# A time-mix and expert-mix block on one core: weights split in place, a new load order ahead of the routed experts, and a combination cut in two

## What is computed

```
mod = (silu(c) @ wmod).reshape(4, 6, 1, -1); sa, ca, ga, sb, cb, gb = six parts   # ga, gb kept away from 0
h  = layernorm(x) * (1 + ca) + sa
x  = x + ga * attn(h)
h  = layernorm(x) * (1 + cb) + sb
x  = x + gb * ffn(h)

attn: time mix    xr, xk, xv = mixes of LN(h) and LN(h) one row earlier
                  r = sigmoid(xr @ Wr); k = xk @ Wk; v = xv @ Wv;  h += (r * exp(u+k)*v / (exp(u+k)+1e-8)) @ Wout
      channel mix h += sigmoid(x2r @ Wr2) * (relu(x2k @ Wk2)**2 @ Wv2)
ffn:  shared expert  (silu(x Wsg) * (x Wsu)) @ Wsd, hidden width 704
      routed experts 8 of width 352, softmax router, each row goes to its best 2, weighted sum
```

## Time and profile before

| | before |
|---|---|
| median of 3 runs | 1906.12 us (1905.55 to 1906.73) |
| profiled execution, its own time | 1902.73 us |
| its span, first to last instruction | 1901.0 us |
| mean granted TensorE clock in it | 0.956 |
| PE busy / DVE busy / ACT busy / POOL busy | 1726.2 / 1347.9 / 767.5 / 548.4 us |

### The profile page before, as it was taken

One profiled execution on the slowest core, in us unless ns is written; L12 is line 12 of the kernel. 1 busy time (PEld: TensorE's weight loads), 2 busy tenths in 40 slices (PEclk: granted clock), 3 DMA queues, 4 the chain that ended last, 5 costly groups with the idle time before them and its releaser, 6 DMA issues.

```text
span 1901.0 us, 28565 instructions
## 1 busy us (share of the span) xinstructions
PE 1726.2 (91%) x9093; PEld 1494.5 (79%) x9093; DVE 1347.9 (71%) x2468; ACT 767.5 (40%) x1147; POOL 548.4 (29%) x631
## 2 busy tenths in 40 slices
PE   4599999997678999999999884999999999997898
PEld 0488888885567878878878784999999999986888
DVE  4899999984587788777776533667666666756752
ACT  2333333341334545545454212455554545432221
POOL 0344444441354434545545420000000000006620
PEclk8699999999789999999999996999999999999999
DMA  9422222211533434545545786766667676677731
GB/s 333 144 91 88 88 88 88 88 66 67 180 111 124 143 139 150 200 151 192 206 147 183 272 287 187 251 237 242 240 233 251 230 255 230 247 243 246 244 118 45
DMA packets 141362, 338.74 MB, mean 178 GB/s; under 512 B 20649, under 2 KB 20649, under 8 KB 135777
## 3 DMA queue, kind: packets, MB, share of 16 engines
q1 hardware_dynamic: 110592, 250.15, 38.4%
q10 hardware_dynamic: 20448, 54.01, 7.7%
q0 software_dynamic: 10240, 33.56, 5.1%
HBM read 230.14 MB, written 107.53 MB: 178 GB/s over the span
## 4 chain that ended last, share of the span: by engine, by line
PE 65%; DVE 19%; DMA 5%; issue 4%; POOL 3%; ACT 2%; SPq 1%; another core or an unknown queue 0%; DVEq 0%; ACTq 0%; POOLq 0%
PE bank L566 16%; PE bank L567 15%; PE bank L568 15%; DVE mix L1544 6%; PE bank L577 4%; PE bank L2032 4%; PE bank L2034 4%; PE bank L2033 4%; PE bank L2027 2%; DVE xm_lo L1550 1%; DMA base<-xres_rows 1%; ACT xm_hi L1147 1%; POOL diff L1000 1%; DMA stage<-in_w_k 1%; DVE k_lo L1557 1%
## 5 line engine op out<-in xcount | busy, mean ns | idle before, releaser
L566 PE MATMUL bank<-gu_hi,ex_x_hl 128*128 128x352 f32 x1136 | 380.3, 335 | 2.7 <-DVE gu_lo L1810 1.9
L568 PE MATMUL bank<-gu_hi,ex_x_hl 128*128 128x352 f32 x1136 | 368.0, 324 | 0.0
L567 PE MATMUL bank<-gu_lo,ex_x_hl 128*128 128x352 f32 x1136 | 367.9, 324 | 0.0
L1081 POOL DMA_INDIRECT raw<-expert_out_rows,out_slots x64 | 74.2, 1159 | 624.7 <-DMA expert_out_rows<-y_rows 588.4
L1628 DVE TENSOR_TENSOR hid<-bank,sg_t 128x352 f32<-128x352 f32 x142 | 74.0, 521 | 231.6 <-ACT sg_t L1205 225.3
L566 PEld LDWEIGHTS bank<-gu_hi,ex_x_hl 128*128 128x128 f32 x1136 | 215.7, 190 | 3.4 <-DVE gu_lo L1810 2.1
L1544 DVE SCALAR_TENSOR_TENSOR mix<-diff,vecs,h2T 128x128 f32<-128x128 f32 x256 | 160.7, 696 | 80.0 <-POOL diff L1000 80.0
L567 PEld LDWEIGHTS bank<-gu_lo,ex_x_hl 128*128 128x128 f32 x1136 | 215.8, 190 | 0.0
L568 PEld LDWEIGHTS bank<-gu_hi,ex_x_hl 128*128 128x128 f32 x1136 | 215.1, 189 | 0.0
L2032 PE MATMUL bank<-dn_hi,hid_hi 128*128 128x512 f32 x426 | 172.7, 405 | 23.5 <-DVE hid_lo L1632 17.2
L1205 ACT ACTIVATE sg_t<-bank 128x352 f32<-128x352 f32 x142 | 66.1, 465 | 306.8 <-PE bank L568 290.7
(11 more groups left out here) (229 smaller groups left out, 3942.0 us busy)
## 6 DMA issues: line engine op xcount, KB each, us to landing
raw<-in_ex_gu SPq DMA_DIRECT2D x39, 1408.0 KB, 6.6
raw<-in_ex_dn SPq DMA_DIRECT2D x39, 512.0 KB, 7.4
ex_x<-expert_in_rows SPq DMA_DIRECT2D x78, 256.0 KB, 2.7
expert_out_rows<-y_rows ACTq DMA_DIRECT2D x78, 256.0 KB, 5.4
h_rows<-h_t SPq DMA_DIRECT2D x64, 256.0 KB, 2.4
h_turned<-h_hl ACTq DMA_DIRECT2D x32, 512.0 KB
ex_x_hl<-h_turned ACTq DMA_DIRECT2D x32, 512.0 KB
x_t<-in_x SPq DMA_DIRECT2D x32, 256.0 KB, 2.6
```

Source lines behind the costliest of these rows:

```text
L566: pe.matmul(acc, act_hi[i], w_hi[i], start=(i == 0), stop=False)
L567: pe.matmul(acc, act_hi[i], w_lo[i], start=False, stop=False)
L568: last = pe.matmul(acc, act_lo[i], w_hi[i], start=False, stop=(i == chunks - 1))
L1081: pool.indirect_dma_start(rows[:, pair % 2, a, :], None, ys_d, bass.IndirectOffsetOnAxis(ap=out_slots[:, k, n:n + 1], axis=0)).then_inc(ar ...
```

## The change

Four things change.

**The opening.** Weights are no longer staged: each is loaded to the place of its own low part (`plain[w]` lies where `w_*_lo` lies), ACT writes the high part, and DVE subtracts in place. So no weight waits for a buffer, and the splits are spread: DVE splits r and k in step -2 of the time mix, v in step -1, o in step 0, and the three channel weights and the router's in steps 3 to 5. The modulation rows are spread too: GA and SB in step -4, CB in step 0, GB in step 1. PE's r no longer waits for all splits. SP's order of loads is new.

**Ahead of the routed stage** SP issues the first expert before the pads, and the first rows right behind the pads; the second expert and the 14 base loads follow.

**In the routed stage** SP's steps are written out instead of looped, and the base and residual loads (28 of 256 KB) go one into each step.

**The combination** is cut in two: `weighted` (both, gated) stands ahead of DVE's `hid` of the half, `combined` (the residual) stays behind it; everything is one tile later. ACT's order is the same.

```diff
 def combined_at(q):
-    return SPLIT + 1 + q // 2, q % 2
+    return SPLIT + 2 + q // 2, q % 2
...
             for i in range(2, len(W1)):
-                load_weight(i)
-            sp.wait_ge(mod_out, 32)
-            for b in range(B):
-                sp.dma_start(flat(mod1[:, b]), mod_d[b, 0:2 * D].partition_broadcast(P)).then_inc(mod1_in, 16)
...
+            sp.wait_ge(mod_out[0], 32)
+            load_mod1(0)
+            load_weight(2)
+            load_weight(3)
+            for b in range(1, B):
+                load_mod1(b)
+            sp.wait_ge(*lnh_vec.done(0, "scaled"))
+            sp.dma_start(x_t[:, 0, :], x_d[2 * P:3 * P, :]).then_inc(x_in[0], 16)
...
             def scaled(t):

                 batch = t.n // TPB
+                if t.pair is None and t.n < 2:
+                    dve.wait_ge(*((mod1_in, 16) if t.n == 0 else (mod1_later, 16 * (B - 1))))
...
             sp.wait_ge(route_done, 1)
+            load_expert(FIRST)
             sp.wait_ge(pads_zero, 1)
             for e in range(E):
                 pad_rows(e)
-            for first in range(2):
-                load_expert(ROUTED.tile(first))
-            sp.wait_ge(rs_out, 16 * FU)
-            for n in range(FU):
-                if n >= 2:
-                    sp.wait_ge(fb_in[n % 2], 16 * (n // 2))
-                sp.dma_start(base[:, n, :], xres_d[n * P:(n + 1) * P, :]).then_inc(fb_in[n % 2], 16)
...
+            load_rows(FIRST)
+            load_expert(ROUTED.tile(1))
+            sp.wait_ge(rs_out, 16 * FU)
...
+            def time_step_and_weights(t):
+                time_step(t)
+                if t.only(-4):
+                    mod_row(GA)
+                    mod_row(SB)
+                if t.only(-2):
+                    split_lo(0)
+                    split_lo(1)
+                if t.only(-1):
+                    split_lo(2)
+                if t.only(0):
+                    split_lo(3)
+                    raise_u()
+                    mod_row(CB)
+                if t.only(1):
+                    mod_row(GB)
+                if t.pair is None and 3 <= t.n <= 5:
+                    split_lo(t.n + 1)
+                if t.only(5):
+                    split_router()
...
                 for half in range(2):
                     before = LATE.before(t, half)
+                    pairs = [q for q in range(NT // 2) if combined_at(q) == (n, half)]
...
                     hidlo(*before)
+                    for q in pairs:
+                        weighted(q)
                     hid_of(LATE, t, half)
```

More of the change, by code:

```diff
@@ L326, in build @@
         assert first.at <= nc.sbuf_usable_end
-        mod_rows = [ring[0:B, p, :] for ring in (h_t, hh, hin_t) for p in range(2)]
-        gate_sign, gate_neg = xh[0:B, :], flat(diff1[0:B, :, :])
+        mod_rows = [rows[0:B, :] for rows in (z_t, sk_t, vk_t, rw_t, hin_t[:, 0, :], hin_t[:, 1, :])]
         second = Shelf(nc, w1_at)
@@ L438, in build @@
         u_in = sem("u_in")
-        w_in = [sem(f"w_in{i}") for i in range(3)]
-        mod_out = sem("mod_out")
+        w_in = [sem(f"w_in{i}") for i in range(len(W1 + W2))]
+        mod_out = [sem(f"mod_out{i}") for i in range(3)]
         mod1_in = sem("mod1_in")
+        mod1_later = sem("mod1_later")
+        wrt_in = sem("wrt_in")
         mod_t_in = pair_of_sems("mod_t_in")
@@ L920, in routed_step @@
                     load_rows(t.back(-1))
-                if t.real() and t.back(-2).real():
+                if t.back(-2).real():
                     load_expert(t.back(-2))
-                if t.pair is None and t.n in (NJ - 2, NJ - 1):
+                if t.n >= NJ - 2:
                     load_shared_again(t.n - (NJ - 2))
-            sweep(sp, NJ, 2, 0, routed_step)
-            for n in range(SPLIT, NT):
-                load_residual(n)
+                if t.n < FU:
+                    load_base(t.n)
+                elif SPLIT <= t.n < NT:
+                    load_residual(t.n)
+            one_by_one(ROUTED, 0, 0, routed_step)
             for q in range(COMBINED_FIRST):
@@ L1089, in _, with round_weight @@
             act.activation(cT[:], cT[:], ACT.Silu).then_inc(silu_c, 1)
[L1090 to L1096, removed]
+            def round_weight(i):
+                act.wait_ge(w_in[i], 16)
+                act.activation(flat(hi[ORDER[i]][:]), flat(plain[ORDER[i]][:]), ACT.Copy).then_inc(wsplit_hi, 1)
+            round_weight(0)
+            round_weight(1)
             def h1T_of(t):
+                if t.only(0):
+                    act.wait_ge(vec_in, 16 * 9)
                 act.wait_ge(*t1_pe.done(t.n, "turned"))
@@ L1128, in rwhi @@
                 act.activation(flat(rw_hi[:]), PS_TR[:], ACT.Copy).then_inc(rw_act.sem, 1)
-            sweep(act, NT, *in_turn((sk, 1), (sr, 0), (rwhi, 2), (mix_hi, -1), (h1T_of, -2)))
+            lead, lag, time_step = in_turn((sk, 1), (sr, 0), (rwhi, 2), (mix_hi, -1), (h1T_of, -2))
+            def time_step_and_weights(t):
+                time_step(t)
+                for i in {-2: [2], -1: [3], 2: [4], 3: [5, 6]}.get(None if t.pair is not None else t.n, []):
+                    round_weight(i)
+                if t.only(3):
+                    act.wait_ge(wrt_in, 16)
+                    act.activation(wrt_hi, wrt[:], ACT.Copy).then_inc(wsplit_hi, 1)
+            sweep(act, NT, lead, lag, time_step_and_weights)
             wait_h_rows(act)
@@ L1887, in _ @@
                     before = LATE.before(t, half)
+                    pairs = [q for q in range(NT // 2) if combined_at(q) == (n, half)]
+                    if n == SPLIT + 2 and not half:
+                        for k in range(2):
+                            dve.wait_ge(fb_in[k], 16 * len(range(k, FU, 2)))
                     hidlo(*before)
+                    for q in pairs:
+                        weighted(q)
                     hid_of(LATE, t, half)
@@ L1893, in _ @@
                         y_of_unit(*before[1:])
-                    if n == SPLIT + 1 and not half:
-                        for k in range(2):
-                            dve.wait_ge(fb_in[k], 16 * len(range(k, FU, 2)))
-                    pairs = [q for q in range(NT // 2) if combined_at(q) == (n, half)]
                     for q in pairs:
                         if q >= COMBINED_FIRST:
-                            combine(q)
+                            combined(q)
                     if before[0] is LATE and not half:
@@ L1917, in _ @@
                 for c in range(C):
-                    last = pe.matmul(psum[m][0:B, :], cT[:, c, :], wmod[:, c, m * D:(m + 1) * D], start=(c == 0),
+                    last = pe.matmul(psum[MOD_BANK[m]][0:B, :], cT[:, c, :], wmod[:, c, m * D:(m + 1) * D], start=(c == 0),
                                      stop=(c == C - 1))
@@ L1936, in r @@
                     pe.wait_ge(*sr_act.done(t.back(1).n, "sr"))
-                if t.pair is None and t.n == 0:
-                    pe.wait_ge(wsplit_lo, NW + 1)
+                if t.only(0):
+                    pe.wait_ge(wsplit_lo, 2)
+                    pe.wait_ge(mod_vec, MOD_AT[3])
                 pe.wait_ge(*mix_vec.done(t.n, "mix_lo"))
```

135 lines of the change are left out of this document (70 added, 65 removed).

## The result

| | before | after |
|---|---|---|
| median | 1906.42 us (4 runs, 1905.55 to 1907.44) | 1946.16 us (4 runs, 1943.24 to 1949.62) |
| profiled execution's span | 1901.0 us | 1947.9 us |
| mean granted TensorE clock in it | 0.956 | 0.946 |

The change makes the kernel slower by 2.17%, ratio 1.0217 with a 95% interval of 1.0203 to 1.0231, or 39.7 us. The prediction was 1943. The profiled execution, 1949.62 us, is the slowest of the four runs, 3.5 us above their median.

The account below looks back on a forecast made before the run. PE was taken to set the end, so changes count by its gaps. Profiled 1902.7 + 0.7 (opening) - 18.7 (routed stage) + 54.6 (combination) = 1939.3, with 3.4 to the median 1943 us; 8-in-10 range 1914 to 1962.

Parts of the forecast that it names:

- Combination, predicted +54.6 us: Late stage: DVE's hid waits behind weighted, so PE idles in 16 halves; 54.4 idle + 25.6 clock - 25.4 present cost.
- the sum: Whole kernel: profiled 1902.7 us plus the terms of opening, routed stage and combination, 1939.3, or 1943 with 3.4 to the median.
- idle term: Combination: PE idles 3.4 us in each of 16 halves waiting for hid, 54.4 us.
- clock term: Combination: the granted clock falls around each gap, 1.6 us a half, 25.6 us over 16 halves.
- The present cost of 25.4 us: Combination before the change: eight tiles take 125.2 us where 16 plain halves take 99.8, a cost the change removes.
- Start of the routed stage, predicted -18.7: Before the routed stage: PE restarts 21.7 us earlier, at 1143.1, then waits 3.0 us for hid_lo; ends -24 and -13.
- Opening, predicted +0.7: Time mix: first product at 60.0 us, 11.3 earlier, then 12.0 lost as DVE catches up; ends -12 and +5.
- Rival 1: Combination: the clock stays up through the gaps, total 1917 us; chance 0.15.
- Rival 2: Combination: the clock stays down longer, 3.0 us lost a half, total 1965 us; chance 0.10.
- Rival 3: Combination: faster than before; with the first product early PE loses at most 1.6 us a half, 1888 us; chance 0.07.
- Rival 4: Opening: it keeps its lead since DVE's surplus hides, 12 us less, total 1931 us; chance 0.05.
- rival 5: Routed stage: pads behind an expert land late, so rows come no earlier; 15 us more, 1958 us; chance 0.03.

Follow-up runs that it names:

- the run of opening and routed order: The changed kernel with the combination of before, its new opening and routed load order kept: 1891.54 us, ratio 0.9934 to before.
- the first experiment: The changed kernel with one move on ACT, the first product ahead of hid_hi's rounding and silu in each late half: 1867.28 us, ratio 0.9821 to before.
- the combination alone: The kernel before with only the change's combination (later tiles, cut in two around hid): 1955.74 us, ratio 1.0275 to before.
- experiment 11: The run of opening and routed order with the combination one tile later, whole, behind hid: 1884.79 us, ratio 0.9887 to before.
- experiment 10: The run with the splits early, with ACT's rounding of the second expert behind hid_hi and silu in the first routed half: 1862.20 us, ratio 0.9771 to before.
- the run with the splits early: The first experiment's kernel with DVE's splits of w_r and w_k one time step earlier: 1860.50 us, ratio 0.9777 to before.

## Why the prediction was right

- **Combination, predicted +54.6 us.** Alone it measured +50.8 (52.4 by the ratio); the changed kernel less the run of opening and routed order gives +54.6 by the medians and +53.9 by the ratios. The mechanism is shown by the first experiment. Read from turning to turning, the last 26 of the late stage's 28 halves would take 162.4 us without a combination. They take 187.9 before, 241.5 with the combination alone and 248.9 in the changed kernel. So the combination cost 25.5 us (25.4 in the sum) and now costs 79.1 in the one run and 86.4 in the other (80.0 in the sum). The idle term was right, 3.4 us a half at full clock, though PE's wait itself reads 3.2. The clock term was too low, 1.9 for 1.6: in the changed kernel the half came to 11.60 us where the sum said 11.24. That the whole came out so close is in part luck: the clock did not fall alike in every run, and a half took 11.12 us in the run of the combination alone.
- **The present cost of 25.4 us** is one number for two things that the prediction did not tell apart. 8.2 us of it stand in a single half of the kernel before, where `hid_lo` stood behind DVE's first weighting, and that behind the gathered rows:

```profile
1717.12 1.41 DVE L1866 SCALAR_TENSOR_TENSOR raw<-raw,w,raw 128x512 f32<-128x512 f32 x2 [4.06 <-DMA raw<-expert_out_rows,out_slots]
...
1721.66 0.77 PE L2032 MATMUL bank<-dn_hi,hid_hi 128*128 128x512 f32 x1 [6.12 <-issue]
```

  The rest is mostly a wait of 1.7 to 1.8 us for `hid_lo` in every second half. The shift by a tile removes the first whatever the order on DVE, as experiment 11 shows; only the second is the order's.
- **Start of the routed stage, predicted -18.7.** The order alone measured -18.5 (17.0 by the ratio). In its trace PE stands 4.3 us for the rows and 3.6 for `hid_lo` in place of 25.7, 17.8 less. In the changed kernel the restart is at 1145.4, not 1143.1; the wait for `hid_lo` 3.2 us, not 3.0. Its cause was only half right: it is the second expert's late issue, but ACT's queue is not the only road, as experiment 10 shows.
- **Opening, predicted +0.7.** Measured +2.4 at tile 8, within the ends of -12 and +5. First product 61.4 for 60.0, since x tile 2 landed at 43.8 and not 41.8; given back 12.3 for 12.0. The mechanism holds step by step: r of tiles 4 to 8 starts 53.2, 66.6, 80.0, 93.4 and 105.5 us after that of tile 0, where the sum said 52.7, 65.5, 78.9, 92.5 and 105. The vector loads had cost 9.1 us of SP, 9.5 in the sum. Over the whole kernel it is 5.1 us by the medians, which the intervals do not separate from 2.4.
- **Rival 1 (the clock stays up)** is out for the changed kernel: it fell at all 16 gaps. It is true of single gaps, three of the 16 in the run with the combination alone. **Rival 2** is out as a mean, though half of it is true: after seven of the 16 gaps the clock stayed down for 5.5 to 6.1 us from PE's restart, after the other nine for 2.9 to 3.9.
- **Rival 3** named the right place and mis-sized it. It allowed PE 1.6 us a half with the first product early, which gave 1888; the run took 1867, with one long wait left and halves of 6.36 us on average. The step that failed is that 2.65 us of weighting would overshoot the room between `hid_lo` and silu by 1.6: in the run `hid_lo` is through at 1732.68 and the silu at 1735.26, 2.6 us of room, and the weighting ends at 1735.35.
- **Rival 4** is out, since the opening's lead of 9.9 us was gone by tile 8; **rival 5** too, since PE restarted 19.4 us earlier than before.

What stays open: ACT began some operations late with a releaser that the trace does not resolve (3 to 10 us idle around 1700 to 1717 in three of the runs), and how much of the opening's 2 to 5 us lasts to the end.

## What to carry to other kernels

When a piece of work is moved ahead of the operation that an idle engine waits for, its own inputs move on the critical path too: find their producer in its engine's queue, and move that first. The kernel with this cut took 2.2% more or 1.8% less than before, by where one call stood on ScalarE. Of the time gained upstream of a restart that waits for DMA, 6.5 us here, 2.7 were left behind it, so read the next such point before working on the stage ahead of it.

## What the runs showed of the hardware

Gaps of the same length don't leave the clock alike. After PE's gap at 1744.3 to 1747.6 in the changed kernel (3.25 us) it was still at its low level 5 us later, after the one at 1722.2 to 1725.4 (3.25 us too) it was up soon after 1729:

```profile
1729.00:1732.00 3.00, 3.00 (x18) 2.88 (x17) 0.00 (x0) 0.59 (x3) 0.00 (x0) 0.96 0.61 216
...
1750.00:1753.00 3.00, 3.00 (x12) 3.00 (x12) 0.00 (x0) 0.00 (x0) 0.62 (x1) 0.50 0.97 305
```

And one gap of 1.84 us between the routed and the late stage left the clock at 1.00 in the run with the splits early, but in the run with the rounding behind it fell to 0.50:

```profile
1679.00:1681.00 2.00, 2.00 (x13) 2.00 (x14) 0.94 (x2) 0.00 (x0) 0.00 (x0) 1.00 0.00 0
```

```profile
1678.00:1680.00 2.00, 2.00 (x8) 2.00 (x8) 0.00 (x0) 0.00 (x0) 0.00 (x0) 0.50 0.00 0
```

So a run can differ by a few us with no change in its work, and the cost of a gap is better read from many of them than from one.
